# One accumulator bank moved from the ring of the maxima and the solver to the ring of the side work

## The chip, the cores and the metric

One core of one Trainium2 chip runs the whole program. The metric is the device time in microseconds (us) of one execution; three runs of the kernel before gave 1116.82, 1129.46 and 1138.49, so the median is 1129.46. Engines are named as in the profile: PE is the matrix engine (PEld its weight loads), DVE the vector engine, ACT the scalar engine, POOL the general engine, SP the one that issues transfers. PSUM is the memory that PE writes into: eight banks of 128 partitions by 512 fp32 numbers.

## The reference

Three transformer layers on x of shape (2, 512, 144), then a rotation. All are modulated by shifts, scales and gates that come from a condition vector of 144 numbers per batch element.

```
each layer:  h = layernorm(x) * (1 + scale) + shift
             q, k, v = split(h @ w_qkv + b)          # 16 heads of 9 columns
             (layer 1: q and k are layernormed per head and multiplied by a gain)
             x = x + gate * (softmax(q k^T / 3) v @ w_proj + b)
             h = layernorm(x) * (1 + scale) + shift
             x = x + gate * mlp(h)                   # 144 -> 576 -> 144, gelu
             (layer 0: four such mlps, the best two of each token, weighted)
rotation:    U = qr(P).Q  (144 x 64);  R = expm(A(cond))  (64 x 64, skew A)
             x + ((x U) R - x U) U^T
```

## The kernel before

**Blocks, groups, steps.** A block is one layer for one batch element (512 tokens); there are 6, worked on one after the other. A block has 4 groups of 4 heads, a group has 16 steps, so there are 384 steps, numbered n. In a step PE computes the scores of 128 keys against 512 queries for one head (`scores`, L1259, into an `s_bank`), ACT takes the exponential (L664), and every fourth step PE multiplies the probabilities of four heads with v (`pv`, L1291, eight matmul records, in the one `o_bank`).

**Maxima.** The softmax needs the row maximum of the scores one group ahead. For the next group PE computes the scores turned round (`max_scores`, L1270, into an `m_bank`) and DVE reduces them (`take_max`, L824): two in each of the first two steps of a group, then one a step, none in the last two. In step 14 PE turns the maxima (`max_turn`, L1278, four matmuls) and DVE subtracts them from q (`place_max`, L831). Before the turn PE waits until every `m_bank` is drained.

**Solver.** Rows of small linear algebra on 64 x 64 matrices give U and R: parts `gram` and `lu` (63 each), and the parts of the matrix exponential (`taylor`, `square` and a few others). A part is one or a few small matmuls of PE into an `m_bank` (L1476 for `gram` and `lu`, L1488 for `taylor`, L1499 for `square`), then three or four dependent DVE instructions, of which the last drains the bank (`gram`: L1067, L1071, L1074; `lu`: L1095, L1099, L1100, L1102). Each part of a chain waits for the one before. `solver_plan` spreads them over the steps: one `gram` or `lu` every 2.5 steps up to step 295, and from step 141 to 257 one part of the exponential every 4 steps. That makes 146 parts with a bank in 135 steps; in 11 of these steps there are two.

**Side work.** Norms, qkv, projection, gate and the mlps of the neighbouring blocks are cut into slots (`SLOTS`), put between the steps. Their matmuls write `d_bank`s. An mlp takes seven: five for the first matrix (`up`, L1394 to L1397, drained by ACT's second gelu, L734), two for the second (`down`, L1409 to L1419, drained by DVE, L1001 in layer 0). POOL and SP prepare weights and use no bank.

**Rings.** All engines walk through the same two rings of banks in the same order (`Banks.take`). Take number k of a ring with R banks gets bank k mod R, and PE waits until take k - R is drained. The ring of the `m_bank`s serves maxima, turns and solver parts; the ring of the `d_bank`s serves the side work. The eight banks are two `s_bank`s, one `o_bank`, three `m_bank`s and two `d_bank`s.

**Order.** It is written out by hand and the same in every run. PE in step n: maxima, scores(n), the turning of o (step 4 of a group, L1299), pv (steps 2, 6, 10, 14), max_turn (step 14), the slots of n, the solver parts of n. DVE in step n: (step 5: o_normalise, L839 and L842), the slots of n - 1, the solver parts of n - 1, the maxima of n. One maximum may be taken earlier: the first wait inside a slot's norm or a `gram` or `lu` part is filled with it (`fill`, set to `fill_once` while slots and parts run).

Of the kernel before, what the change touches and what calls it, by code (L numbers as in the profile page):

```python
# [41 lines left out]
EPS = 1e-6  # L42
GRP = 4
G = NH // GRP
S_BANKS, M_BANKS, D_BANKS = 2, 3, 2
PROBS = 8
MAXROW = 3 * HD
VW = HD + 1
# [146 lines left out]
def max_tiles(step):  # L195

    at = sum(MAX_SHARE[:step % GSTEPS])
    return [divmod(i, GRP) for i in range(at, at + MAX_SHARE[step % GSTEPS])]
# [26 lines left out]
class Tally:  # L225
# [5 lines left out]
    def next(self, name):  # L231
        self.n[name] = self.n.get(name, 0) + 1
        return self.n[name]


def build(nc, a, out):
    with ExitStack() as ctx:
# [413 lines left out]
        def _(act):  # L651
# [19 lines left out]
            def norm(blk, kind):  # L671
                yield
                (a_bank, _, _), (d_bank, _, _) = ring.take(), ring.take()
                yield
                act.wait_ge(s["h_turned"], T * seen.next("norm"))
                act.activation(h_hi[:, :], a_bank[:, :], ACT.Copy).then_inc(s["h_hi_ready"], 1)
                act.activation(h_d[:, :], d_bank[0:DW, :], ACT.Copy).then_inc(s["h_hi_ready"], 1)
                yield

            def qkv(blk):  # L680
                copied = []
                for slot in range(2 + T):
                    taken = ring.take(), ring.take()
                    if slot < 2:
                        copied += [(drained, before + 1) for _, drained, before in taken]
                        for i, (bk, drained, _) in enumerate(taken):
                            act.wait_ge(s["qkv_full"], seen.next("qkv_full"))
                            act.activation(qkv_tok[:, 2 * slot + i, :], bk[:, 0:3 * C], ACT.Copy).then_inc(drained, 1)
                    else:
                        bk, drained, _ = taken[0]  # L690
                        act.wait_ge(s["stack_turned"], seen.next("stack_turned"))
                        act.activation(q_t[:, blk % 2, :, (slot - 2) * P:(slot - 1) * P],
                                       bk[:, :].rearrange("p (g n) -> p g n", g=G), ACT.Copy).then_inc(drained, 1)
                        bk, drained, _ = taken[1]
                        act.wait_ge(s["stack_turned"], seen.next("stack_turned"))
                        act.activation(k_t[:, blk % 2, :, (slot - 2) * P:(slot - 1) * P],
                                       bk[:, :].rearrange("p (g n) -> p g n", g=G), ACT.Copy).then_inc(drained, 1)
# [89 lines left out]
        def _(dve):  # L787
# [9 lines left out]
            fill = [lambda: None]  # L797
# [23 lines left out]
            def take_max(grp, t, j):  # L821
                bk, drained, _ = mring.take()
                dve.wait_ge(s["max_full"], seen.next("max_full"))
                dve.tensor_reduce(row_max[:, grp % 2, t, MAXROW + 32 * j:MAXROW + 32 * j + 1], bk[:, :], AX.X, ALU.max).then_inc(drained, 1)  # L824

            def place_max(grp):

                bk, drained, before = mring.take()
                q = q_t[:, grp // G % 2, grp % G, :]
                dve.wait_ge(s["max_turned"], grp + 1)  # L830
                dve.scalar_tensor_tensor(out=q, in0=bk[:, :], scalar=-1.0, in1=q.bitcast(F32), op0=ALU.mult,  # L831
                                         op1=ALU.add).then_inc(drained, 1)
                dve.wait_ge(drained, before + 1)

            def o_normalise(grp):

                dve.wait_ge(s["o_turned"], grp + 1)
                view = o_bank[:, :].rearrange("p (t j w) -> p t j w", t=T, j=GRP)
                link(dve.reciprocal(o_rden[:, :, :], view[:, :, :, HD]))  # L839
                g = grp % G  # L840
                dst = o_tok[:, grp // G % 2, :, g * GRP * HD:(g + 1) * GRP * HD].rearrange("p t (j d) -> p t j d", d=HD)
                dve.tensor_tensor(dst, view[:, :, :, 0:HD], o_rden[:, :, :].unsqueeze(3).to_broadcast([P, T, GRP, HD]),  # L842
                                  ALU.mult).then_inc(s["o_taken"], 1)
# [347 lines left out]
            for n in range(BLOCKS * STEPS + 1):  # L1191
                grp = n // GSTEPS
                if n % GSTEPS == 5 and grp > 0:
                    o_normalise(grp - 1)
                maxima = list(max_tiles(n)) if grp + 1 < BLOCKS * G else []

                def next_max():

                    if maxima:
                        take_max(grp + 1, *maxima.pop(0))  # L1200

                def fill_once():
                    if len(maxima) == len(max_tiles(n)):
                        next_max()

                if n:

                    taken = [mring.take() if part[0] in SOLVER_BANK else None for part in SOLVER_PLAN[n - 1]]
                    fill[0] = fill_once
                    for _ in range(SLOTS[n - 1]):  # L1210
                        next(woven)
                    for part, banks in zip(SOLVER_PLAN[n - 1], taken):
                        solver(part, banks)
                    fill[0] = lambda: None
                while maxima:
                    next_max()
                if n % GSTEPS == TURN_AT and grp + 1 < BLOCKS * G:
                    place_max(grp + 1)
# [351 lines left out]
```

## Time and profile before

| | |
|---|---|
| runs | 1116.82, 1129.46, 1138.49 us; median 1129.46 us |
| the profiled execution | 1115.3 us; its span 1113.6 us, so 1.7 us lie around it |
| PE busy | 913.7 us, 82% of the span |
| DVE busy | 647.9 us, 58% |
| ACT busy | 413.2 us, 37% |
| mean granted clock of PE | 0.619 of full |
| transfers | 15.98 MB, mean 14 GB/s |

The span is the time from the first to the last instruction. A matmul's end is modelled, and PE pipelines its matmuls, so its busy share holds some overlap: four L1270 and L1259 rows that start in the same moment run beside each other on different rows of the array. A wait row says which engine and line waited for which engine's line, its sum, its count and its longest. Where a row of the timeline has `<-`, the number ahead of it is the idle time before it, and the name what ended that.

### The profile page before, as it was taken

How to read it: one execution, taken by the hardware profiler on the slowest of the kernel's cores; microseconds unless marked ns; L12 is line 12 of the kernel's file. 1: busy time of each engine (PE TensorE's matmuls, PEld its weight loads, DVE VectorE, ACT ScalarE, POOL GpSimd, SP SyncE). 2: the span in 40 equal slices, each digit the busy share in tenths (PEclk: the TensorE clock that was granted, in tenths of full speed). 3: DMA queues.
4: the chain of work that ended last, by engine and by line, in shares of the span. 5: the costliest groups of instructions: out<-in, count | busy, mean ns of one | idle time of the engine just before them, and what ended most of it. 6: DMA issues, size and time to landing. Idle time of an engine off the chain costs nothing.

```text
span 1113.6 us, 11687 instructions
## 1 busy us (share of the span) xinstructions
PE 913.7 (82%) x3794; PEld 501.5 (45%) x3794; DVE 647.9 (58%) x1753; ACT 413.2 (37%) x742; POOL 200.2 (18%) x351
## 2 busy tenths in 40 slices
PE   5578998979997798896976896978887879989847
PEld 1433443446753334675534343635433544335326
DVE  4177656665458767624478667466766465575233
ACT  0303543325433442433334331426332445536412
POOL 4201133012311102224211004011003020021020
PEclk9855655558976555567765555657555765658656
DMA  3000010000110000111100000000000100000000
GB/s 106 14 1 22 10 31 16 25 7 17 44 49 0 1 1 0 31 30 30 45 1 0 1 1 11 20 1 1 1 1 1 31 0 1 1 1 1 11 0 11
DMA packets 22022, 15.98 MB, mean 14 GB/s; under 512 B 6427, under 2 KB 19391, under 8 KB 21962
## 3 DMA queue, kind: packets, MB, share of 16 engines
q1 hardware_dynamic: 21914, 15.22, 5.0%
q8 instruction: 31, 0.51, 0.2%
q14 instruction: 29, 0.24, 0.1%
q10 hardware_dynamic: 48, 0.02, 0.0%
HBM read 14.62 MB, written 0.61 MB: 14 GB/s over the span
## 4 chain that ended last, share of the span: by engine, by line
PE 63%; DVE 25%; ACT 4%; issue 4%; POOL 2%; DMA 0%; SPq 0%; DVEq 0%; ACTq 0%; POOLq 0%
PE m_bank L1270 12%; PE o_bank L1291 12%; DVE row_max L824 7%; PE s_bank L1259 3%; PE d_bank L1352 3%; PE d_bank L1409 2%; PE m_bank L1476 2%; PE d_bank L1411 2%; PE m_bank L1278 2%; PE d_bank L1410 2%; PE d_bank L1308 2%; PE d_bank L1309 2%; PE d_bank L1323 2%; PE d_bank L1241 2%; PE d_bank L1394 2%
## 5 line engine op out<-in xcount | busy, mean ns | idle before, releaser
L664 ACT ACTIVATE probs<-s_bank 128x512 f32<-128x512 f32 x384 | 220.7, 596 | 492.2 <-PE s_bank L1259 488.9
L824 DVE TENSOR_REDUCE row_max<-m_bank 128x1 fp32r<-128x512 f32 x384 | 256.2, 687 | 162.6 <-PE m_bank L1270 158.1
L1270 PE MATMUL m_bank<-k_t,q_t 32*128 32x512 f32 x384 | 216.6, 741 | 59.4 <-DVE lu L1102 21.3
L1259 PE MATMUL s_bank<-q_t,k_t 32*128 32x512 f32 x384 | 237.5, 736 | 6.4 <-ACT probs L664 5.6
L1291 PE MATMUL o_bank<-probs,v_aug 128*32 128x512 f32 x768 | 175.8, 1007 | 4.0 <-DVE o_tok L842 3.0
L1270 PEld LDWEIGHTS m_bank<-k_t,q_t 32*128 32x128 f32 x384 | 81.7, 267 | 163.8 <-issue 51.4
L1259 PEld LDWEIGHTS s_bank<-q_t,k_t 32*128 32x128 f32 x384 | 89.2, 267 | 29.5 <-ACT probs L664 16.2
L590 POOL TENSOR_TENSOR h_tok<-h_tok,mod 128x144 f32<-128x144 f32 x48 | 24.3, 507 | 273.3 <-DVE h_tok L883 273.3
L983 DVE TENSOR_TENSOR g_lo<-g_raw,g_hi 128x512 fp32r<-128x512 f32 x48 | 37.6, 792 | 37.4 <-ACT g_hi L734 37.2
L1409 PE MATMUL d_bank<-ff_hi,g_hi 128*128 128x144 f32 x192 | 57.1, 297 | 1.3 <-ACT g_hi L734 1.0
L1411 PE MATMUL d_bank<-ff_lo,g_hi 128*128 128x144 f32 x192 | 56.7, 295 | 0.0
L1410 PE MATMUL d_bank<-ff_hi,g_lo 128*128 128x144 f32 x192 | 56.6, 295 | 0.0
L1323 PE MATMUL d_bank<-ident,h_tok 128*128 128x128 f32 x80 | 33.9, 427 | 18.8 <-POOL h_tok L594 18.8
L608 POOL TENSOR_TENSOR qs_tok<-qkv_tok,qs_tok 128x144 fp32r<-128x144 f32 x24 | 11.9, 495 | 206.2 <-ACT ks_tok L713 206.2
L593 POOL COPY h_tok<-o_tok 128x144 f32<-128x144 f32 x24 | 7.4, 308 | 230.8 <-DVE o_tok L842 205.2
L1278 PEld LDWEIGHTS m_bank<-ident_r,row_max 128*128 128x128 f32 x96 | 21.8, 317 | 57.4 <-issue 34.3
L732 ACT ACTIVATE g_raw<-d_bank 128x512 f32<-128x512 f32 x60 | 36.0, 600 | 30.8 <-PE d_bank L1397 24.7
L1394 PE MATMUL d_bank<-h_hi,ff_hi 128*128 128x512 f32 x60 | 33.9, 566 | 15.8 <-ACT g_hi L734 6.9
L1409 PEld LDWEIGHTS d_bank<-ff_hi,g_hi 128*128 128x128 f32 x192 | 40.3, 210 | 5.6 <-ACT g_hi L734 5.0
L1278 PE MATMUL m_bank<-ident_r,row_max 128*128 128x128 f32 x96 | 26.1, 422 | 20.3 <-DVE q_and_gram L1074 5.8
L831 DVE SCALAR_TENSOR_TENSOR q_t<-m_bank,q_t 128x512 fp32r<-128x512 f32 x24 | 16.6, 691 | 43.7 <-PE m_bank L1278 43.7
L1411 PEld LDWEIGHTS d_bank<-ff_lo,g_hi 128*128 128x128 f32 x192 | 40.7, 212 | 0.0
(239 smaller groups left out, 1559.0 us busy)
## 6 DMA issues: line engine op xcount, KB each, us to landing
raw_a<-in_L_cond_w_dram SPq DMA_DIRECT2D x20, 288.0 KB
raw_a<-in_L_cond_W_fc_dram SPq DMA_DIRECT2D x4, 288.0 KB
w_rows<-in_L_cond_W_dram SPq DMA_DIRECT2D x8, 141.8 KB
raw_d<-in_L_cond_w_dram SPq DMA_DIRECT2D x30, 36.0 KB
raw_a<-in_L_cond_w_dram SPq DMA_DIRECT2D x20, 36.0 KB
x_tok<-in_x_dram SPq DMA_DIRECT2D x2, 288.0 KB, 4.3
out_dram<-moe SPq DMA_DIRECT2D x4, 144.0 KB, 1.9
raw_d<-in_L_cond_w_dram SPq DMA_DIRECT2D x30, 4.0 KB
```

What stands on the lines that cost most here:

```text
L664: act.activation(probs[:, n % PROBS, :], s_banks[n % S_BANKS][:, :], ACT.Exp, scale=HD ** -0.5)\
L824: dve.tensor_reduce(row_max[:, grp % 2, t, MAXROW + 32 * j:MAXROW + 32 * j + 1], bk[:, :], AX.X, ALU.max).then_inc(drained, 1)
L983: dve.tensor_tensor(g_lo[:, f, :], g_raw[:, (n - 1) % 2, :], g_hi[:, f, :].bitcast(F32), ALU.subtract).then_inc(s["g_lo_ready"], 1)
L1259: pe.matmul(s_banks[n % S_BANKS][:, :], k_t[rows, par, g, kt * P:(kt + 1) * P], q_t[rows, par, g, :], start=True, stop=True).then_inc(s["s ...
L1270: pe.matmul(bk[:, :], q_t[rows, par, g, t * P:(t + 1) * P], k_t[rows, par, g, :], start=True, stop=True).then_inc(s["max_full"], 1)
L1278: ins = pe.matmul(bk[:, t * P:(t + 1) * P], row_max[:, grp % 2, t, :], ident_r[:, :], start=True, stop=True)
L1291: ins = pe.matmul(o_bank[32 * j:32 * j + 32, :], v_aug[:, par, kt, at:at + 32], probs[:, (GRP * quad + j) % PROBS, :], start=(kt == 0), st ...
L1323: pe.transpose(a_bank[:, cols], h_tok[:, t, 0:P], ident[:, :])
L1394: pe.matmul(bk[:, :], ff_hi[:, i, c], h_hi[:, :], start=True, stop=False)
L1409: pe.matmul(dst, g_hi[:, f, cols], ff_hi[:, i, w], start=(f == 0), stop=False)
L1410: pe.matmul(dst, g_lo[:, f, cols], ff_hi[:, i, w], start=False, stop=False)
L1411: pe.matmul(dst, g_hi[:, f, cols], ff_lo[:, i, w], start=False, stop=False)
```

## The change

It changes two numbers and one line. The ring of the maxima and the solver has two banks in place of three, the ring of the side work three in place of two. The early maximum (`fill_once`) is allowed only in steps in which fewer solver parts than `M_BANKS` wait to be finished, that is, in which there are no two. All sizes, loops and matmuls stay.

```
-S_BANKS, M_BANKS, D_BANKS = 2, 3, 2
+S_BANKS, M_BANKS, D_BANKS = 2, 2, 3
...
                     taken = [mring.take() if part[0] in SOLVER_BANK else None for part in SOLVER_PLAN[n - 1]]
-                    fill[0] = fill_once
+                    if sum(banks is not None for banks in taken) < M_BANKS:
+                        fill[0] = fill_once
```

Lines after the changed one stand one lower in the kernel after (L1270 becomes L1271). PE's instructions keep their order; only the banks differ.

First place: PE around two `gram` parts in the first block, each between maxima and scores. Before:

```order
L1476 MATMUL m_bank2<-q_and_gram,ident 64x65
L1270 MATMUL m_bank0<-k_t,q_t 128x512
L1259 MATMUL s_bank1<-q_t,k_t 128x512
L1270 MATMUL m_bank1<-k_t,q_t 128x512
L1259 MATMUL s_bank0<-q_t,k_t 128x512
L1299 MATMUL o_bank<-ident,o_t 128x128 x4
L1476 MATMUL m_bank2<-q_and_gram,ident 64x65
L1270 MATMUL m_bank0<-k_t,q_t 128x512
L1259 MATMUL s_bank1<-q_t,k_t 128x512
L1270 MATMUL m_bank1<-k_t,q_t 128x512
L1259 MATMUL s_bank0<-q_t,k_t 128x512
L1291 MATMUL o_bank<-probs,v_aug 32x512 x4
```

The same stretch of the change:

```order
L1477 MATMUL m_bank0<-q_and_gram,ident 64x65
L1271 MATMUL m_bank1<-k_t,q_t 128x512
L1260 MATMUL s_bank1<-q_t,k_t 128x512
L1271 MATMUL m_bank0<-k_t,q_t 128x512
L1260 MATMUL s_bank0<-q_t,k_t 128x512
L1300 MATMUL o_bank<-ident,o_t 128x128 x4
L1477 MATMUL m_bank1<-q_and_gram,ident 64x65
L1271 MATMUL m_bank0<-k_t,q_t 128x512
L1260 MATMUL s_bank1<-q_t,k_t 128x512
L1271 MATMUL m_bank1<-k_t,q_t 128x512
L1260 MATMUL s_bank0<-q_t,k_t 128x512
L1292 MATMUL o_bank<-probs,v_aug 32x512 x4
```

Before, the second maximum behind a part has a bank that the part does not hold, and only the third comes back to the part's; now the second maximum has the part's own bank.

Second place: PE from the end of one mlp of layer 0 to the start of the next one. Before:

```order
L1418 MATMUL d_bank1<-ff_lo,g_hi 128x144
L1419 MATMUL d_bank1<-ff_d,ones_r 128x144
L1270 MATMUL m_bank1<-k_t,q_t 128x512
L1259 MATMUL s_bank1<-q_t,k_t 128x512
L1476 MATMUL m_bank2<-q_and_gram,ident 64x65
L1270 MATMUL m_bank0<-k_t,q_t 128x512
L1259 MATMUL s_bank0<-q_t,k_t 128x512
L1291 MATMUL o_bank<-probs,v_aug 32x512 x4
L1394 MATMUL d_bank0<-h_hi,ff_hi 128x512
L1395 MATMUL d_bank0<-h_lo,ff_hi 128x512
```

The same stretch of the change:

```order
L1419 MATMUL d_bank2<-ff_lo,g_hi 128x144
L1420 MATMUL d_bank2<-ff_d,ones_r 128x144
L1271 MATMUL m_bank0<-k_t,q_t 128x512
L1260 MATMUL s_bank1<-q_t,k_t 128x512
L1477 MATMUL m_bank1<-q_and_gram,ident 64x65
L1271 MATMUL m_bank0<-k_t,q_t 128x512
L1260 MATMUL s_bank0<-q_t,k_t 128x512
L1292 MATMUL o_bank<-probs,v_aug 32x512 x4
L1395 MATMUL d_bank0<-h_hi,ff_hi 128x512
L1396 MATMUL d_bank0<-h_lo,ff_hi 128x512
```

Before, the first `up` of the next mlp has the bank of the first `down`, which DVE drains late; now it has the bank of the last `up`, and the two `down` banks are 1 and 2.

Third place: DVE in one of the steps with two parts (an `lu` and a `taylor`), as a piece of the difference, before with -, after with +:

```order
 L824 TENSOR_REDUCE row_max<-m_bank 128x1 x3
 L1095 TENSOR_SCALAR s_small<-m_bank 64x1
-L824 TENSOR_REDUCE row_max<-m_bank 128x1
 L1099 RECIPROCAL s_small<-s_small 64x1
 L1100 SCALAR_TENSOR_TENSOR s_small<-lu,s_small,neg_after 64x1
 L1102 SCALAR_TENSOR_TENSOR lu<-m_bank,s_small,lu 64x43
 L1140 SCALAR_TENSOR_TENSOR rot<-m_bank,ident 64x2x64
-L824 TENSOR_REDUCE row_max<-m_bank 128x1 x2
+L824 TENSOR_REDUCE row_max<-m_bank 128x1 x3
```

The maximum that was taken inside the `lu` part is now taken behind both parts.

## Rows read from the trace of the kernel before

**Rows 1.** The page: busy time of each engine, then the last chain by engine.
```profile
PE 913.7 (82%) x3794; PEld 501.5 (45%) x3794; DVE 647.9 (58%) x1753; ACT 413.2 (37%) x742; POOL 200.2 (18%) x351
...
PE 63%; DVE 25%; ACT 4%; issue 4%; POOL 2%; DMA 0%; SPq 0%; DVEq 0%; ACTq 0%; POOLq 0%
```

**Rows 2.** Waits of PE: for whom, sum in us, times, longest.
```profile
PE m_bank L1270 <- DVE lu L1102: 21.3, 12, 4.0
PE d_bank L1323 <- POOL h_tok L594: 18.8, 9, 6.6
PE m_bank L1270 <- DVE row_max L824: 18.1, 25, 3.7
...
PE m_bank L1270 <- DVE q_and_gram L1074: 13.8, 7, 5.7
...
PE d_bank L1394 <- ACT g_hi L734: 6.9, 13, 2.7
PE d_bank L1394 <- DVE moe L1001: 6.1, 3, 4.6
...
PE d_bank L1308 <- DVE moe L1001: 3.0, 2, 2.1
```

**Rows 3.** Waits of all engines: ACT's gelu behind the up matmuls.
```profile
ACT g_raw L732 <- PE d_bank L1397: 24.7, 32, 4.3
```

**Rows 4.** Groups by line, PE: operation, shapes, count; busy, mean ns; idle before.
```profile
L1476 PE MATMUL m_bank<-q_and_gram,ident 64*64 64x65 f32 x126 | 28.4, 324 | 5.1 <-DVE q_and_gram L1074 5.0
...
L1476 PE MATMUL m_bank<-lu,ident 64*64 64x64 f32 (+62 forms) x126 | 25.2, 288 | 16.4 <-DVE lu L1102 16.3
```

**Rows 5.** Timeline of PE from 181.4 us: start, length, line, operation.
```profile
181.45 0.48 PE L1476 MATMUL m_bank<-q_and_gram,ident 64*64 64x65 f32 x2
181.86 0.79 PE L1270 MATMUL m_bank<-k_t,q_t 32*128 32x512 f32 x1
181.86 0.79 PE L1259 MATMUL s_bank<-q_t,k_t 32*128 32x512 f32 x1
181.87 0.79 PE L1270 MATMUL m_bank<-k_t,q_t 32*128 32x512 f32 x1
181.87 0.79 PE L1259 MATMUL s_bank<-q_t,k_t 32*128 32x512 f32 x1
182.59 1.11 PE L1299 MATMUL o_bank<-ident,o_t 128*128 128x128 f32 x4
184.83 0.45 PE L1476 MATMUL m_bank<-q_and_gram,ident 64*64 64x65 f32 x2 [1.12 <-DVE q_and_gram L1074]
185.21 0.79 PE L1270 MATMUL m_bank<-k_t,q_t 32*128 32x512 f32 x1
...
185.46 0.79 PE L1270 MATMUL m_bank<-k_t,q_t 32*128 32x512 f32 x1
...
186.19 1.94 PE L1291 MATMUL o_bank<-probs,v_aug 128*32 128x512 f32 x8
188.05 0.79 PE L1270 MATMUL m_bank<-k_t,q_t 32*128 32x512 f32 x1
```

**Rows 6.** Timeline of DVE, same stretch.
```profile
182.68 0.69 DVE L824 TENSOR_REDUCE row_max<-m_bank 128x1 fp32r<-128x512 f32 x1 [0.56 <-PE m_bank L1270]
...
184.41 0.28 DVE L1074 SCALAR_TENSOR_TENSOR q_and_gram<-m_bank,s_small,q_and_gram 64x64 f32<-64x64 f32 x1
...
185.61 0.31 DVE L842 TENSOR_TENSOR o_tok<-o_bank,o_rden 128x144 f32<-128x144 f32 x1
...
186.04 0.69 DVE L824 TENSOR_REDUCE row_max<-m_bank 128x1 fp32r<-128x512 f32 x1
...
186.88 0.28 DVE L1074 SCALAR_TENSOR_TENSOR q_and_gram<-m_bank,s_small,q_and_gram 64x64 f32<-64x64 f32 x1
```

**Rows 7.** Windows: stretch, its length, busy PE, PEld, DVE, ACT, POOL, clock, transfers.
```profile
181.40:188.80 7.40, 6.28 (x31) 2.63 (x27) 5.13 (x12) 2.77 (x5) 2.88 (x3) 0.50 0.01 1
...
355.60:370.10 14.50, 6.87 (x30) 4.71 (x26) 13.20 (x45) 5.59 (x13) 2.01 (x5) 0.50 0.00 1
...
200.00:310.00 110.00, 98.08 (x453) 63.09 (x454) 62.06 (x148) 48.30 (x80) 28.02 (x32) 0.71 0.09 23
```

## The prediction

> **What bounds the kernel now.** I read the page first: PE is busy for 82% of the span, DVE for 58%, and the chain that ended last runs 63% over PE and 25% over DVE [rows 1]. So PE sets the pace, and what costs time is where PE, which takes its instructions in order, stands still. The waits of PE come next, because they say which ring of banks is the tighter one. The maxima (L1270) stand 21.3, 18.1 and 13.8 us behind DVE's last instruction of an `lu` part, DVE's own maxima and the last instruction of a `gram` part, 53.2 us in all [rows 2]. A maximum has no other input from these, so these are waits for an `m_bank`, and that with three of them. In the other ring, the waits that a bank can explain are those of the first up matmul behind the gelu (6.9 us) and behind `moe`, the drain of the down banks (6.1 us), and of the modulation matmul behind `moe` (3.0 us): 16.0 us in all [rows 2]. The 18.8 us of L1323 behind POOL are data and no bank [rows 2]. The change takes a bank from the ring that costs three times as much and gives it to the other.
>
> **The change, its second ring first.** With three `d_bank`s the first up matmul of an mlp no longer needs the bank of the first down matmul, and PE can be one bank further ahead of ACT. At most the 16.0 us go. Below that, nothing: the bank is asked for anyway, ACT needs two gelus a bank whatever PE does, and a PE that is early waits at the next bank. I take 10 us off, since the 6.1 and 3.0 us come from DVE being late with a drain that is now a whole bank away, and the 6.9 us are spread over 13 waits, each of which comes back in part.
>
> **The first ring.** With R banks PE may start take k when take k - R is drained. The order on PE around a solver part is: part, maximum, scores, (pv or a slot), maximum. With three banks the second maximum needs only the bank of a maximum that was taken before the part. With two it needs the part's own bank. That bank is free when DVE has done the whole part, and inside the part DVE first takes the maximum between (the fill), so the wait holds a maximum's way through PE and DVE as well. PE has nothing else to do meanwhile: the scores of the step, the turning of o, pv and the next part all stand behind the waiting maximum in its order, and ACT waits for the scores.
>
> I worked this through on a stretch with two `gram` parts and no side work.
> - The first part starts at 181.45; its last DVE instruction ends at 184.41 + 0.28 = 184.69 [rows 5, 6]. The second maximum, which started at 181.87 beside the first, now starts at 184.69, and its scores with it.
> - The turning of o came 182.59 - 181.87 = 0.72 behind the maximum [rows 5], so now at 185.41. The second part follows after its 1.11 us, at 186.53 instead of 184.83; part of the delay is eaten here, since PE stood 1.12 us before this part anyway, for the drain of the first [rows 5]. So it is 1.70 late.
> - The third maximum comes 0.38 behind it, at 186.91, ready 0.79 later, at 187.70 [rows 5]. DVE, whose o_normalise (end at 185.92 before) moves with the turning of o, is free by then. From the start of this maximum on DVE to the end of the part it took 186.88 + 0.28 - 186.04 = 1.12 [rows 6]. The part is drained at 188.82.
> - The fourth maximum, at 185.46 before, starts there: 3.4 late. pv and the fifth maximum (188.05 before) [rows 5] have only PE's own work ahead of them and are 3.4 late too.
>
> Two parts, 3.4 us: 1.7 us a part, in a stretch where PE was busy for 6.28 of 7.40 us and DVE for 5.13 [rows 7]. I did not find anything later that gives this back, since DVE is 69% busy there and waits for PE in its turn.
>
> How many parts are like these? `gram` and `lu` make 252 matmul records, two a part [rows 4], so 126 parts; with those of the exponential, and without the 16 ahead of the first step, the plan has 146 in 135 steps. From the tables of slots and parts: in 24 of the 135 steps the two steps behind bring no second maximum (the end of a group). In 24 there is a pv between the maxima and in 29 a slot with side work. A pv alone takes 1.94 us [rows 5] and covers the wait, which from the start of the second part to its drain was 187.16 - 184.83 = 2.33. There remain 58 steps with nothing between, 15 of them at the start of a group, where two maxima stand next to each other. 58 x 1.7 = 99 us.
>
> The bounds of a part's price: nothing where DVE is the slower one. From 355.6 to 370.1 DVE is busy for 13.2 of 14.5 us and PE for 6.87 [rows 7]: there PE only waits earlier for what it waits for anyhow. At most 1.7 us also for the 53 parts that I take as covered: 111 x 1.7 = 189. I take the 58, since DVE's 58% over the span [rows 1] is nearer to the first stretch's 69% than to the other's 91%.
>
> **The fill.** In the 11 steps with two parts the maximum is now taken behind both. With two banks it must be: PE cannot compute it before the first part is drained. A maximum on DVE takes 0.69 us [rows 6] that used to lie inside the part's waits; I count 0.8 us for each, with the gap, 9 us. Bounds: none, or 11 x 1.7 = 19.
>
> **Sum.** 99 + 9 - 10 = 98 us more. The profiled execution took 1115.3 us, so it would take 1213. It lies 14 us below the median of the runs, 1129.5, and the same 98 us on that give 1227.
>
> **Rivals.**
> *The waits only come forward.* PE waited 53.2 us for `m_bank`s before [rows 2]. If each new wait merely takes the place of one that stood a maximum later, as the 1.12 us did in the stretch above, then of 99 + 9 us only 108 - 53 = 55 are new, and with the full 16 and the like in the other ring some 39 remain: about 1168 us; where DVE bounds more of the time, down to 1145. For it: the rows of 355.6 to 370.1. Against it: in the stretch that I followed the 1.7 us are what is left after that.
> *The side ring pays more.* ACT's first gelu waits 24.7 us for the up matmuls [rows 3]. If the third bank keeps PE ahead, these go beside the 16.0 us: 41 us less, 1129 - 41 = 1088, faster. It decides if the maxima cost under 41 - 23 = 18 us, 11 steps' worth of the 58. Against it: the up matmuls are PE's own work, and PE is the busy one in that stretch, 98 of 110 us [rows 7].
> *The clock falls.* From 200 to 310 us, in the mlps of layer 0, PE's mean granted clock is 0.71, in the stretches without side work 0.50, the lower level of 1.2 GHz [rows 7]. If the added stops brought the first down to the second, 98 us of PE work would take 98 x 0.71 / 0.50 = 139, 41 us more, and twice that for the two elements: 82 us, 1227 + 82 = 1309. Against it: an mlp's matmuls run in one slot with no take of an `m_bank` between, and the stretch followed above is at 0.50 already, where nothing is to be lost.
> The Trainium skill, "TensorE: Matmul & The Clock Gate", section "A second HAM failure mode: psum-queue depth-cycling", tells of a kernel that goes round its PSUM banks with short stops of PE between groups of matmuls, so that the clock went up and down and throughput fell; by that rule the time would be nearer to this rival's. The trace agrees so far as the mean of 0.71 is a mix of both levels; it does not show that bank waits are the reason.
>
> **Chances.** My forecast 0.70; the waits only come forward 0.14; the clock falls 0.11; the side ring pays 0.05. The range goes from 1150 us, which holds most of the first rival, to 1310, which holds the clock's case and three fifths of the way to the upper bound of 189 + 19 us (1337). A measurement of this kernel can tell about 2% from no change, that is 1107 to 1152 us. Slower by over 2%: 0.70 + 0.11 + half of 0.14, 0.88. Within 2%: the other half and a little of the side ring's case, 0.08. Faster: 0.04.
>
> **What would show it.** In the profile of the changed kernel the waits of the maxima (then L1271) for DVE's `lu`, `gram` and maxima rows, 53.2 us before, should be 130 us or more. The waits of the first up matmul for `moe` should be gone and those for the gelu small. ACT's wait for the scores should grow by about the whole difference. The stretch of the two `gram` parts should show the second maximum starting at the drain of the part, and the next pv over 3 us later against the first part than the 4.74 us of before. The clock of the mlps of layer 0 should still be near 0.7. The forecast is wrong if the maxima's waits grow by less than 40 us, or if they grow and the span does not, which would mean that DVE or ACT had the time to give.

## The result, and the profile after

The changed kernel takes 1235.89 us (median of four runs, 1225.48 to 1241.28) against 1133.43 us for the kernel before (median of four, 1116.82 to 1138.49): a ratio of 1.099 with a 95% interval of 1.083 to 1.116, so slower by a tenth. Medians are of all runs, while ratios, here and below, go by the fast runs alone (without 1137.39 and 1138.49 us of the kernel before), so a ratio is not the quotient of the medians beside it. The forecast was 1227 us, in a range from 1150 to 1310. In the two profiled executions the step is 1225.48 - 1115.30 = 110.2 us, and both spans lie within 1.8 us of these times, so the traces show all of it.

The page of the changed kernel, busy time of each engine and the last chain by engine:

```profile
PE 939.9 (77%) x3794; PEld 511.9 (42%) x3794; DVE 654.9 (54%) x1753; ACT 414.0 (34%) x742; POOL 200.3 (16%) x351
...
PE 61%; DVE 30%; issue 4%; ACT 4%; POOL 1%; DMA 0%; DVEq 0%; SPq 0%; ACTq 0%; POOLq 0%
```

Against [rows 1], the same work takes DVE, ACT and POOL about the same time (DVE 7.0 us more, ACT 0.8), and DVE's part of the last chain grows from 25% to 30%. PE is busy for 26.2 us longer (939.9 - 913.7), and it stands still for 283.8 us (1223.7 - 939.9) where it was 199.9 us before (1113.6 - 913.7): 83.9 us more. 26.2 + 83.9 = 110.1 us is the growth of the span.

The 26.2 us come from the maxima and the scores. PE's busy time with these 768 matmuls alone, taken together, over the whole run (stretch, its length, busy PE, mean granted clock, transfers), before and after:

```profile
0.00:1113.60 1113.60, 262.06 (x768) 0.62 0.05 14
0.00:1223.70 1223.70, 287.00 (x768) 0.61 0.05 13
```

They fill 287.0 - 262.1 = 24.9 us more, mainly because fewer of them run beside each other: a single one takes 748 and 743 ns in the mean, where it took 741 and 736. The time in which PE is busy and none of them runs is 913.7 - 262.1 = 651.6 us before and 939.9 - 287.0 = 652.9 us after, the same.

The waits of PE in the changed kernel (for whom, sum in us, times, longest), which answer to [rows 2]:

```profile
PE m_bank L1271 <- DVE lu L1102: 70.9, 39, 6.1
PE m_bank L1271 <- DVE q_and_gram L1074: 49.6, 29, 8.2
PE m_bank L1271 <- DVE row_max L824: 43.6, 63, 6.6
PE d_bank L1324 <- POOL h_tok L594: 18.5, 8, 6.6
PE m_bank L1477 <- DVE row_max L824: 12.8, 21, 1.2
...
PE d_bank L1395 <- ACT g_hi L734: 0.2, 1, 0.2
```

The three rows of the maxima hold 70.9 + 49.6 + 43.6 = 164.1 us, where they held 53.2 [rows 2]: 110.9 us more. The waits for the end of a `gram` or `lu` part are 68 (39 + 29) in place of 19, with 120.5 us in place of 35.1; the waits for another maximum are 63 in place of 25. In the other ring the waits for `moe` are gone, and those for the gelu are down from 6.9 to 0.2 us. That the maxima's waits grow by more than PE's standing still is because others shrank: those of the side ring just named (16.0 us down to 0.2), and the 16.3 and 5.0 us that PE stood ahead of an `lu` or `gram` part for the part before it [rows 4]. No wait row shows these two any more; in their place PE stands there for a maximum, 12.8 us (L1477 <- `row_max`), since the part now wants the bank of a maximum taken shortly before.

The waits of ACT and DVE, of the kernel before:

```profile
ACT probs L664 <- PE s_bank L1259: 488.9, 244, 19.5
DVE row_max L824 <- PE m_bank L1270: 158.1, 138, 13.2
```

and of the changed kernel:

```profile
ACT probs L664 <- PE s_bank L1260: 620.5, 286, 21.7
DVE row_max L824 <- PE m_bank L1271: 243.3, 219, 10.3
```

ACT waits 131.6 us longer for scores, DVE 85.2 us longer for maxima: both engines that PE feeds get their work later, and neither becomes the bound.

**Where in the run.** Windows of the kernel before (stretch, its length, busy PE, PEld, DVE, ACT, POOL, mean granted clock, transfers): ahead of step 0; steps 0 to 303, with all solver parts that are spread over steps; the rest; and steps 64 to 95, with mlps of layer 0.

```profile
0.00:77.50 77.50, 47.85 (x130) 25.79 (x130) 33.52 (x108) 13.71 (x31) 21.26 (x66) 0.80 0.16 43
77.50:938.80 861.30, 726.49 (x3044) 402.52 (x3044) 531.80 (x1466) 329.90 (x590) 157.36 (x233) 0.60 0.05 14
938.80:1113.60 174.80, 139.34 (x622) 73.15 (x622) 82.54 (x180) 69.62 (x122) 21.57 (x52) 0.65 0.01 4
...
200.90:337.60 136.70, 120.17 (x549) 75.38 (x548) 77.09 (x194) 53.87 (x88) 30.60 (x37) 0.71 0.10 29
```

The same stretches of the changed kernel:

```profile
0.00:79.70 79.70, 49.43 (x129) 26.12 (x129) 34.11 (x108) 13.70 (x31) 21.21 (x66) 0.79 0.15 42
79.70:1046.60 966.90, 753.50 (x3043) 414.65 (x3044) 536.84 (x1467) 330.57 (x590) 157.67 (x233) 0.58 0.05 12
1046.60:1223.70 177.10, 137.01 (x623) 71.14 (x623) 83.90 (x180) 69.68 (x122) 21.45 (x52) 0.68 0.01 4
...
225.90:377.00 151.10, 126.83 (x548) 82.00 (x548) 78.56 (x193) 53.32 (x88) 32.18 (x42) 0.66 0.10 26
```

Ahead of the first step 2.2 us are added, behind the last part 2.3, and between them 966.9 - 861.3 = 105.6. The price is paid where parts stand between the steps, and hardly elsewhere: the rest has two `m_bank`s as well, and is 2.3 us longer.

**The stretch of the prediction.** PE around the two `gram` parts of [rows 5], now from 201.28 us:

```profile
201.28 0.47 PE L1477 MATMUL m_bank<-q_and_gram,ident 64*64 64x65 f32 x2
201.69 0.79 PE L1271 MATMUL m_bank<-k_t,q_t 32*128 32x512 f32 x1
...
203.69 0.79 PE L1271 MATMUL m_bank<-k_t,q_t 32*128 32x512 f32 x1 [1.21 <-DVE q_and_gram L1074]
...
205.46 0.47 PE L1477 MATMUL m_bank<-q_and_gram,ident 64*64 64x65 f32 x2
...
207.86 0.79 PE L1271 MATMUL m_bank<-k_t,q_t 32*128 32x512 f32 x1 [1.21 <-DVE q_and_gram L1074]
...
208.58 1.94 PE L1292 MATMUL o_bank<-probs,v_aug 128*32 128x512 f32 x8
210.45 0.79 PE L1271 MATMUL m_bank<-k_t,q_t 32*128 32x512 f32 x1
```

DVE in the first of these parts:

```profile
201.79 0.16 DVE L1067 RECIPROCAL s_small<-m_bank 64x1 f32<-64x1 f32 x1 [1.58 <-PE m_bank L1477]
202.51 0.69 DVE L824 TENSOR_REDUCE row_max<-m_bank 128x1 fp32r<-128x512 f32 x1 [0.56 <-PE m_bank L1271]
203.12 0.20 DVE L1071 SCALAR_TENSOR_TENSOR s_small<-q_and_gram,s_small,neg_after 64x1 f32<-64x1 f32 x1
203.36 0.28 DVE L1074 SCALAR_TENSOR_TENSOR q_and_gram<-m_bank,s_small,q_and_gram 64x64 f32<-64x64 f32 x1
```

This is what was foretold: the second maximum (203.69) starts when the part's last DVE instruction ends (203.36 + 0.28 = 203.64), 2.41 us behind the part, where it was 0.42 before [rows 5]. Of these 1.99 us PE stands still for 1.21; in the rest the first maximum and its scores run without the second pair, which ran beside them before [rows 5]. Of the 2.36 us that the part holds its bank, 203.12 - 201.95 = 1.17 go into DVE's wait for the first maximum and its reduction, between L1067 and L1071. The second `gram` part does it again. pv is now 208.58 - 201.28 = 7.30 us behind the first part, 2.56 later than its 4.74 [rows 5].

### The profile page after: what moved, and what is told of

The parts are those of the page before. It is cut to its first block, busy times and chain, and to the rows that moved or that the text cites. A ratio compares the mean times of both kernels' runs of the same rounds, so it can differ in the third digit from the quotient of the medians.

```text
span 1223.7 us, 11664 instructions
## 1 busy us (share of the span) xinstructions
PE 939.9 (77%) x3794; PEld 511.9 (42%) x3794; DVE 654.9 (54%) x1753; ACT 414.0 (34%) x742; POOL 200.3 (16%) x351
## 4 chain that ended last, share of the span: by engine, by line
PE 61%; DVE 30%; issue 4%; ACT 4%; POOL 1%; DMA 0%; DVEq 0%; SPq 0%; ACTq 0%; POOLq 0%
PE m_bank L1271 16%; PE o_bank L1292 12%; DVE row_max L824 11%; PE d_bank L1353 3%; PE s_bank L1260 2%; PE m_bank L1279 2%; PE d_bank L1410 2%; PE d_bank L1309 2%; PE d_bank L1310 2%; DVE s_small L1100 2%; PE d_bank L1412 2%; PE d_bank L1411 2%; PE d_bank L1242 2%; PE d_bank L1324 1%; PE m_bank L1477 1%
## 5 line engine op out<-in xcount | busy, mean ns | idle before, releaser
L664 ACT ACTIVATE probs<-s_bank 128x512 f32<-128x512 f32 x384 | 223.2, 596 | 622.4 <-PE s_bank L1260 620.5
L824 DVE TENSOR_REDUCE row_max<-m_bank 128x1 fp32r<-128x512 f32 x384 | 258.7, 688 | 247.2 <-PE m_bank L1271 243.3
L1271 PE MATMUL m_bank<-k_t,q_t 32*128 32x512 f32 x384 | 249.9, 748 | 172.4 <-DVE lu L1102 70.9
L1260 PE MATMUL s_bank<-q_t,k_t 32*128 32x512 f32 x384 | 252.2, 743 | 3.0 <-ACT probs L664 2.6
L1271 PEld LDWEIGHTS m_bank<-k_t,q_t 32*128 32x128 f32 x384 | 91.6, 269 | 304.4 <-DVE lu L1102 88.7
L1260 PEld LDWEIGHTS s_bank<-q_t,k_t 32*128 32x128 f32 x384 | 92.2, 268 | 17.4 <-ACT probs L664 8.0
L1411 PEld LDWEIGHTS d_bank<-ff_hi,g_lo 128*128 128x128 f32 x192 | 38.6, 201 | 0.4
L561 POOL TENSOR_TENSOR ff_lo<-raw_a,ff_hi 128x1360 fp32r<-128x1360 f32 x12 | 37.0, 3087 | 7.5 <-issue 6.7
```

The source lines that it names most:

```text
L561: pool.tensor_tensor(lo[:, 0:na], raw_a[:, 0:na], hi[:, 0:na].bitcast(F32), ALU.subtract)\
L664: act.activation(probs[:, n % PROBS, :], s_banks[n % S_BANKS][:, :], ACT.Exp, scale=HD ** -0.5)\
L1260: pe.matmul(s_banks[n % S_BANKS][:, :], k_t[rows, par, g, kt * P:(kt + 1) * P], q_t[rows, par, g, :], start=True, stop=True).then_inc(s["s ...
L1271: pe.matmul(bk[:, :], q_t[rows, par, g, t * P:(t + 1) * P], k_t[rows, par, g, :], start=True, stop=True).then_inc(s["max_full"], 1)
L1411: pe.matmul(dst, g_lo[:, f, cols], ff_hi[:, i, w], start=False, stop=False)
```

## The experiments

My theory: the price is the ring of the maxima, whose second maximum behind a part waits for the part's own bank; the third `d_bank` gives next to nothing back; the fill rule is small. The rivals: the side ring or the fill rule carries a good part of it; only the maximum inside the part makes the wait dear; or it is the mix of two kinds of work in one ring, and not the number of banks.

### The parts of the change, one at a time

Two banks in either ring, the eighth bank left unused:

```
-S_BANKS, M_BANKS, D_BANKS = 2, 2, 3
+S_BANKS, M_BANKS, D_BANKS = 2, 2, 2
```

> The changed kernel with two banks in the side ring instead of three; the eighth bank is left unused. Theory A (the loss is the maxima's ring, the third side bank gives back a little): 5 to 15 us above the changed kernel, 1241 to 1251 us, and the waits of the first up matmul for the gelu and for moe, gone in the changed kernel, back at 10 to 20 us. Rival B (the side ring's third bank, which lets side work run ahead, is part of the loss): below the changed kernel by 10 us or more.

Measured: 1234.81 us against 1123.84, ratio 1.105 (1.097 to 1.114). It and the changed kernel ran again side by side:

> Two banks in either ring once more, in five rounds beside the changed kernel. Theory A: 0 to 10 us above the changed kernel; in the stretch of layer 0's mlps (steps 64 to 192) more of it than elsewhere. If it is below the changed kernel or within 3 us, the prediction's 10 us for the third side bank were too many.

> The changed kernel itself, on the same chip as the kernel with two side banks, in five rounds, to tell what the third side bank is worth. Theory A (the removed waits for side banks, 16 us, come back in part as other waits): 0 to 10 us below the kernel with two and two banks.

Measured: 1236.29 us without the third `d_bank`, ratio 1.101 (1.096 to 1.106), and 1237.44 us with it, ratio 1.101 (1.095 to 1.106). A gain from the third `d_bank` is not to be seen; the 10 us forecast would be 0.9%. The waits of PE in the kernel without it say why:

```profile
PE d_bank L1395 <- ACT g_hi L734: 4.1, 14, 1.1
...
PE d_bank L1309 <- DVE moe L1001: 0.3, 1, 0.3
```

4.1 + 0.3 = 4.4 us are left of the 16.0 us of [rows 2], with two `d_bank`s as before; 10 to 20 us were expected. A PE that comes later finds most banks drained anyway. The vanished waits of the side ring in the changed kernel are thus for the greater part no work of the third bank.

The fill rule alone, with the banks as before:

```
-                    fill[0] = fill_once
+                    if sum(banks is not None for banks in taken) < 2:
+                        fill[0] = fill_once
```

> The kernel before with the new rule alone: no maximum is taken ahead in a step with two solver parts; the rings stay at three and two banks. Theory A: 0 to 9 us above the kernel before (11 steps, at most 0.8 us each), 1130 to 1142 us, not to be told from no change. Rival B (the rule makes much of the loss, since it holds back maxima where the solver is densest): 30 us or more above.

Measured: 1118.09 us against 1123.84, ratio 0.997 (0.986 to 1.007). No loss is to be seen; the 9 us that I had put on the rule would be 0.8%, just beyond the interval. So the tenth belongs to the ring of the maxima, to within about one per cent of the time.

### The maximum inside the part

If the wait is dear because DVE takes a maximum inside the part, it should fall once DVE does not. In both kernels no maximum is taken ahead inside a part (inside the norms it still is):

```
                         next(woven)
+                    fill[0] = lambda: None
                     for part, banks in zip(SOLVER_PLAN[n - 1], taken):
                         solver(part, banks)
-                    fill[0] = lambda: None
```

> The changed kernel, with no maximum taken inside any solver part (inside the norms of the side work it stays). A part then holds its bank for about 1.2 us instead of 2.3, and the second maximum behind it waits some 0.3 us instead of 2.0. Theory A (the price is the bank's time in the part, with the maximum inside it): 50 to 95 us below the changed kernel, 1140 to 1185 us, and the maxima's waits for the last DVE instruction of gram and lu fall from 120 us to under 50. Rival C (the price is that PE can be only two takes ahead of DVE at all, whatever is inside the part): within 20 us of the changed kernel.

> The kernel before, three and two banks, with no maximum taken inside any solver part: what taking the fill away does by itself. Theory A: within 15 us of the kernel before, 1115 to 1148 us; a gain is possible, since here too maxima wait 35 us for the end of a part. Rival C: slower by 20 us or more, because DVE then stands idle between the dependent instructions of a part.

Measured: with two `m_bank`s 1176.91 us, ratio 1.052 (1.044 to 1.061); with three 1095.61 us, ratio 0.979 (0.971 to 0.987). Both gain, the one with two banks twice as much, but 81.3 us remain between them. Waits of PE with two banks:

```profile
PE m_bank L1271 <- DVE lu L1102: 40.0, 30, 6.3
PE m_bank L1271 <- DVE row_max L824: 39.8, 58, 7.2
PE m_bank L1271 <- DVE q_and_gram L1074: 30.5, 15, 9.3
```

Waiting for the end of a part has gone from 120.5 to 70.5 us, less far than expected (under 50). With three banks and the same edit the three rows hold 17.7 (maxima), 11.5 and 8.4 us. In the stretch of the two `gram` parts the first part of the two-bank kernel starts at 192.81 us, and the second maximum behind it 1.28 us later:

```profile
194.09 0.79 PE L1271 MATMUL m_bank<-k_t,q_t 32*128 32x512 f32 x1
```

So in this stretch 2.41 - 1.28 = 1.13 us of the delay are the maximum inside the part; the part's own three DVE instructions, from 193.32 to 194.04 us, make most of the rest.

The three-bank kernel is faster than the kernel before: a maximum taken ahead inside a part costs time even there. Is it the part alone? The fill goes altogether, in both:

```
-                    fill[0] = fill_once
```

(in the changed kernel the `if` above it too).

> The kernel before, three and two banks, with no maximum taken ahead anywhere, in the parts or in the side work's norms. With the parts' fill gone the kernel took 1096 us. If a maximum taken ahead costs because it lengthens the time that a bank is held, the norms, which hold no m_bank, should gain from their fill: 0 to 15 us above 1096. If taking ahead costs by itself, it is below 1096.

> The changed kernel, two and three banks, with no maximum taken ahead anywhere. It gives the price of the third bank where nothing is taken ahead: the kernel with three and two banks took 1084 us so. If the lengthened part is the larger half of the loss, as the runs without the parts' fill say (1177 against 1096 us), this is 1155 to 1175 us, and 70 to 90 us of price remain: the wait of the second maximum for a part of 1.2 us. If the early maximum were all of it, about 1084 to 1100 us.

Measured: with three banks 1083.50 us against 1125.71, ratio 0.964 (0.959 to 0.970); with two 1176.81 us against 1120.07, ratio 1.053 (1.048 to 1.059). With three banks the time lies below the 1096 us, which speaks for a maximum taken ahead costing time in the norms too. That is not firm: 0.964 and 0.979 were not measured side by side, and their intervals almost touch; and with two banks the norms' fill cost nothing (1.053 without it, 1.052 with it). The three-bank kernel is the fastest of all, faster than both that were compared; the two-bank one lies just above the 1155 to 1175 us expected. Between two and three banks there are still 1.0535 - 0.9645 = 0.089 of some 1,124 us, 100 us, so most of the price of a bank does not need the fill. Waits of PE with two banks and no fill:

```profile
PE m_bank L1269 <- DVE row_max L824: 57.4, 61, 7.2
PE m_bank L1269 <- DVE lu L1102: 34.7, 29, 6.5
...
PE m_bank L1269 <- DVE q_and_gram L1074: 19.2, 10, 5.7
```

With three banks and no fill the same rows are 31.3, 6.6 and 10.0 us. What the parts no longer hold, the maxima do, which DVE now reduces behind the part: 57.4 us for `row_max`. Of the 92.2 us between these two profiled spans (1172.8 and 1080.6), PE stands still for 50.1 and is busy for 42.1 longer (952.2 against 910.1): here too, part of the price is maxima and scores that no longer run beside each other.

Why does the fill cost, with three banks? Most of what it cost lies in steps 144 to 255: 26.2 us of the 33.0 between the two profiled spans (1113.6 and 1080.6). DVE's waits for a maximum in these steps, in the kernel before:

```profile
DVE row_max L824 <- PE m_bank L1270: 48.8, 50, 13.2
```

and without the fill:

```profile
DVE row_max L824 <- PE m_bank L1269: 29.9, 13, 8.7
```

DVE stood still 50 times for a maximum, mostly for half a microsecond to one; now 13 times. One of the 50, DVE around an `lu` part of the kernel before:

```profile
504.22 0.69 DVE L824 TENSOR_REDUCE row_max<-m_bank 128x1 fp32r<-128x512 f32 x1 [0.50 <-PE m_bank L1270]
504.94 0.15 DVE L1099 RECIPROCAL s_small<-s_small 64x1 f32<-64x1 f32 x1
```

The maximum was put into the gap of a dependent chain before PE had it ready, and the chain's next instruction, which needed nothing from it, started 0.5 + 0.7 us late. In these steps DVE's waits for a maximum are 18.9 us shorter, of 26.2 us in all. That they are the cause is argued and not shown: in the other steps the same waits shrank by 24.6 us (in all from 158.1 to 114.6) and the time by 6.8 only.

### Is it the mix or the number?

Maxima (with their turns) and solver parts get a ring each. First out of the same two banks, one each, with three `d_bank`s; then out of three, two for the maxima and one for the parts, with two `d_bank`s. Both keep the rule of no fill with two parts.

```
+MAX_BANKS = 1        # 2 in the second
...
         def ring_m():
-            return Banks(m_banks, m_drained)
+            return Banks(m_banks[:MAX_BANKS], m_drained[:MAX_BANKS])
+
+        def ring_s():
+            return Banks(m_banks[MAX_BANKS:], m_drained[MAX_BANKS:])
```

> The changed kernel's banks, two for maxima and solver and three for the side work, but as two rings of one: one bank for maxima and turns, one for the solver parts. A maximum then waits for the maximum before it, never for a part. Theory A (the loss comes from a maximum that needs a part's bank): 30 to 80 us below the changed kernel, 1155 to 1205 us, since the maximum between is drained some 0.5 us before the part that it is taken in, and where no part is near, one bank makes PE and DVE take turns. Rival C (two banks are too few, however they are shared): as slow as the changed kernel or slower.

> The kernel before's banks, three and two, but as two rings: two banks for maxima and turns, one for the solver parts; no early maximum in steps with two parts. Theory A: the maxima's waits for the end of gram and lu (35 us before) go, so 5 to 35 us below the kernel before, 1098 to 1128 us. Rival C (the banks' number decides, not what a maximum shares its bank with): within 5 us of the kernel before or above it.

Measured: one and one 1309.54 us against 1123.70, ratio 1.166 (1.159 to 1.174); two and one 1139.12 us, ratio 1.015 (1.007 to 1.024). Both missed what my theory expected and came out as the rival C of these runs had it. Waits of PE with one and one:

```profile
PE m_bank L1275 <- DVE row_max L828: 193.4, 222, 6.0
```

No maximum waits for a part any more, but each waits for the one ahead of it, in steps without a part too: from step 296 on, where hardly any parts are left, this kernel loses 58 us, the changed one 3. With two and one:

```profile
PE m_bank L1275 <- DVE row_max L828: 33.0, 57, 3.8
PE m_bank L1493 <- DVE lu L1106: 31.0, 10, 10.3
...
PE m_bank L1504 <- DVE lu L1106: 25.4, 12, 7.4
```

Here too no maximum waits for a part. But the parts of the exponential (L1493, L1504) now stand for 56.4 us behind an `lu` part that holds the one bank, and the scores behind them with it. So the mix is not the fault: three banks are needed, two for maxima that stand together and one for a part. Whether a common ring hands them out better than a fixed share is not clear: the four runs with two and one go from 1126.75 to 1146.24 us.

### Scores ahead of the maxima

If what hurts is that ACT's scores stand behind a waiting maximum in PE's order, then scores, the turning of o and pv should go first. The edit is the same in both kernels:

```
-                if grp + 1 < BLOCKS * G:
-                    for t, j in max_tiles(n):
-                        max_scores(grp + 1, t, j)
                 scores(n)
...
                     pv(n // GRP - 1)
+                if grp + 1 < BLOCKS * G:
+                    for t, j in max_tiles(n):
+                        max_scores(grp + 1, t, j)
```

> The changed kernel, with PE's order in a step altered: scores, turning of o and pv ahead of the maximum, so that they no longer stand behind a maximum that waits for its bank. Theory A (the price is what stands behind the waiting maximum in PE's order): 20 to 60 us below the changed kernel, 1175 to 1215 us, with ACT's wait for the scores smaller by about as much. Rival D (DVE and the solver's chain set the pace, so the maximum only comes later and with it the part it is taken in): same as the changed kernel or slower.

> The kernel before with the same order of PE: scores, turning of o and pv ahead of the maximum. Theory A: up to 20 us below the kernel before, 1113 to 1133 us. Rival D: slower, by what the maxima come later, pv's 1.94 us in every fourth step, up to 40 us.

Measured: two banks 1297.24 us, ratio 1.153 (1.147 to 1.159); three 1203.32 us, ratio 1.070 (1.064 to 1.076). Both are worse, by 60 and 80 us, than with the maxima first. Waits of DVE and ACT in the first:

```profile
ACT probs L664 <- PE s_bank L1260: 622.2, 251, 21.7
DVE row_max L824 <- PE m_bank L1271: 348.0, 259, 10.4
```

ACT waits as long as in the changed kernel (620.5 us), but DVE 105 us longer for its maxima. With three banks DVE's wait grows too, to 265.2 us from 158.1. But PE stands still for no longer than before the edit: 1294.9 - 1026.4 = 268.5 us against 283.8. What grows is its busy time, from 939.9 to 1026.4 us, and most of that in the maxima and scores, which in this order run less beside each other. The two together, over the whole run, with two banks and with three:

```profile
0.00:1294.90 1294.90, 365.09 (x768) 0.58 0.05 12
0.00:1197.40 1197.40, 318.95 (x768) 0.60 0.05 13
```

They fill 365.1 - 287.0 = 78.1 us more with two banks, where the span grew by 71.2, and 319.0 - 262.1 = 56.9 more with three, where it grew by 83.8. So the edit changed more than the order of the waits. Whether late scores or late maxima do the harm stays open: these two runs neither show nor refute the part of my theory that puts it on the late scores.

## Why the prediction was right, step by step

**The place and the mechanism were right.** The maxima's waits came to 164.1 us (130 or more were named), the second maximum starts at the part's drain, ACT's wait for scores grew by more than the whole difference, and the runs with one part of the change at a time leave the tenth to the ring of the maxima.

**The price of a part (1.7 us) was too high in the stretch; the sum came out near because costs that it does not name made up for it.** In the stretch the two parts made pv 2.56 us late, not over 3: 1.3 us a part. The failed step is the drain of the first part. I read it off the trace as 3.24 us behind the part, and 1.08 of it was an L1071 which in the changed kernel, without the POOL instruction beside it, took 0.20 us: an accident of that place (over its 63 times the line took 0.30 us in the mean), which I gave to all parts. At 1.3 us, the 58 parts would have made 75 us. Over the whole run PE waits 49 times more for the end of a part (68 against 19), with 120.5 - 35.1 = 85.4 us more, 1.7 us each; that is the length of a wait and not what a part makes pv late, so that it equals the forecast's 1.7 proves nothing. The 38 added waits for other maxima, with 25.5 us, have no term in my sum at all. I read them as the follow-up: a maximum that starts at the drain of a part is reduced later, and the next maximum but one wants its bank; no run isolates this. Of the 110.9 us of both, 27.0 are taken back by waits that shrank elsewhere (83.9 us of standing still are left), and PE's maxima and scores, which run less beside each other, add 24.9 us, which the sum does not name either. 99 us were predicted for steps with parts; 105.6 us came between step 0 and step 304. That these are so near is in part luck.

**The third `d_bank` (-10 us) was a miss: no gain is to be seen**, 1.1005 with it and 1.1011 without, each to about 0.006. The failed step is that I took the waits of before as a saving in the kernel after. The bank was asked for late enough there without it.

**The fill rule (+9 us) was a miss, too,** with 0.997 (0.986 to 1.007). The failed step is deeper than the term: I took it for granted that a maximum inside a part's gaps is hidden work. With three banks it is a loss: 28 us inside the parts (1123.84 - 1095.61), and perhaps 12 in the norms (1095.61 - 1083.50, not measured side by side).

Both misses have opposite signs and left the sum where it was: 98 us predicted, 102.5 between the first medians, 111.7 in the repeat (1237.44 - 1125.71), which is nearer to what the ratio of 1.099 says.

**The rivals.** *The waits only come forward* is refuted: PE stands still for 83.9 us more, where this rival gave 39 at most after what the side ring saves. *The side ring pays more* is refuted by the runs without the third `d_bank`. *The clock falls* is true in direction and small: in the mlps of layer 0 the mean granted clock went from 0.71 to 0.66, not to 0.50, and PE was busy for 126.83 - 120.17 = 6.7 us longer there; over the whole span it went from 0.619 to 0.607 (in the repeat it was 0.597 to 0.607 against 0.612 to 0.636). Outside the maxima and scores PE's busy time did not grow (651.6 and 652.9 us), and the 7 ns by which each of the 768 became longer are 5 us at most, so over the run the clock cost little. The rule of the Trainium skill that I set beside this rival ("TensorE: Matmul & The Clock Gate", section "A second HAM failure mode: psum-queue depth-cycling") says that short stops at PSUM banks make the clock go up and down and cost throughput; here such stops tripled, from 53.2 to 164.1 us, and the mean clock of the profiled executions gave way by 2%. One sum of the chances was off: 1310 lies three quarters of the way from the forecast of 1227 to the upper bound of 1337, not three fifths; nothing hangs on it.

## What to carry to other kernels

Where an engine that works in order takes banks from one ring for two kinds of work, count the banks that each kind holds at once: here it took one for the kind that holds it long and two for the kind that comes in pairs, and one bank fewer made this kernel a tenth slower, while a third bank in a ring whose waits were 16.0 us in all brought nothing to be seen. A wait on an engine that works in order can cost twice: here PE stood still, and it also lost the running of two matmuls beside each other, which shows as busy time. Before a dependent chain's gap is filled with other work, look at whether that work is ready when the gap opens: in the trace, an idle time ahead of the filling instruction is time that the chain may lose. And before a duration from one stretch is multiplied, compare it with the line's mean over the whole run.

## What the hardware showed that I had not expected

A 64 x 1 instruction of DVE, which takes 0.20 us elsewhere (L1071 at 203.12 above), can take over 2 us beside an instruction of POOL. Timeline of the kernel before, two places:

```profile
182.97 1.39 POOL L567 TENSOR_TENSOR lay_d<-raw_d,lay_d 32x576 fp32r<-32x576 f32 x1
183.29 1.08 DVE L1071 SCALAR_TENSOR_TENSOR s_small<-q_and_gram,s_small,neg_after 64x1 f32<-64x1 f32 x1
...
504.60 3.06 POOL L561 TENSOR_TENSOR ff_lo<-raw_a,ff_hi 128x1360 fp32r<-128x1360 f32 x1
505.13 2.54 DVE L1100 SCALAR_TENSOR_TENSOR s_small<-lu,s_small,neg_after 64x1 f32<-64x1 f32 x1
```

POOL's instructions end at 184.36 and 507.66, DVE's at 184.37 and 507.67: DVE's ends with POOL's, both times. The Trainium skill, "SBUF — State Buffer", section "Who interferes with whom", says that a DVE instruction with two SBUF inputs contends with a GpSimd (here POOL) instruction that reads SBUF, since its second input comes through a read interface that the two share; both places agree with it. So do two instructions that were not stretched: L824, which reads PSUM and took its usual 0.69 us beside the same L567 [rows 6], and L1099 with its one SBUF input, 0.15 us beside L561 (its row stands with the runs without the fill).

PE's maxima and scores that start in one moment run beside each other [rows 5]. Where the maximum waits, this is lost: the groups of the maxima and the scores show 249.9 and 252.2 us of busy time in the changed kernel, 216.6 and 237.5 before, for the same 384 instructions each, and both together 287.0 us in place of 262.1. That is 24.9 of the 26.2 us that PE was busy longer. A bank that comes free late thus shows in the profile as busy time too, and not only as a wait.
